# A wider product for the high softmax weights of a block's first query tile, with its low part added by VectorE

## The chip, the cores and the metric

The kernel runs on one core of a Trainium2 chip. The metric is the device time of one execution in microseconds (us); three executions of the kernel before took 2311.84, 2314.03 and 2314.23 us, so its median is 2314.03 us. A further execution was recorded by the profiler, and all durations below are from it: 2309.51 us, of which 2307.7 us lie between the first and the last instruction (the span).

## The reference: what must be computed

One decoder layer with the normalisation behind each part: self-attention, cross-attention, and a feed-forward part. The cross-attention is nearly all of the work, and the change lies in it:

```python
qh = _split_heads(jnp.einsum('bnq,qi->bni', x, Wq))        # 8 heads of 128, 16*112 = 1792 queries
kh = _split_heads(jnp.einsum('bmc,ci->bmi', context, Wk))  # 16*375 = 6000 keys
vh = _split_heads(jnp.einsum('bmc,ci->bmi', context, Wv))
sim = jnp.einsum('hid,hjd->hij', qh, kh) * SCALE
mean = jnp.mean(sim, axis=-1, keepdims=True)
sim = (sim - mean) * ATTN_MATRIX_SCALE + mean
attn = jax.nn.softmax(sim, axis=-1)
out = jnp.einsum('hij,hjd->hid', attn, vh)
```

The heads are split so that all batches of a head stand in one sequence: every one of a head's 1792 queries attends to all 6000 keys.

## The kernel before, in words

**Precision.** Values in float32 are written as a sum of two halves in float16, a high one and a low one. A product of two such values is three products on TensorE: high by high, high by low, low by high, all summed in PSUM. So the scores take `k_hi` by `q_hi`, `k_hi` by `q_lo` and `k_lo` by `q_hi` (line 416), and the output takes the softmax weights' high half `e_hi` by V's high half, `e_hi` by V's low half, and `e_lo` by V's high half (lines 440, 442 and 444).

**Tiling.** A head's queries are cut into 7 blocks of 256 (8 heads, so 56 blocks), a block into 2 query tiles of 128 (`t` is 0 and 1). The 6000 keys are 47 tiles of 128 (the last one of 112), taken in 12 groups `s` of four (three in the last). One group of one block is a step `f`: there are 672.

**One key tile of V** is a row of `VW` = 257 columns for each key: 128 of the high half, one column of ones (these 129 are `OW`), and 128 of the low half. The column of ones makes the sum of the weights come out as column 128 of the output. The output of a block stands in one PSUM bank, 4 or 5 by turns: two areas of 129 columns. For each key tile and each query tile TensorE loads `e_hi` and streams V's 129 high columns, loads `e_hi` again and streams V's 128 low columns into the first 128 columns of the same area, loads `e_lo` and streams the 129 high columns: 3 weight loads and 3 products, 386 columns.

**The pipeline of a step.** In step (n, s) TensorE first makes the scores of the step that lies 17 ahead (12 products of 256 columns, into one of two pairs of banks), then, in some steps, a side task (part of K, V or Q of the next head or block, lines 549, 559 and 566; at s = 8 the transposes and the spreading of the row maxima, lines 643 and 652), and then the attention products of its own step. ScalarE copies the scores into a ring in SBUF (line 839), later takes their exponential (line 854), and for even steps writes `e_hi` as well (line 846). VectorE folds the scores into a running maximum (line 1074, from PSUM) and subtracts the row maxima in the ring, 4 steps ahead (line 1095). GpSimd writes `e_hi` for odd steps (line 1596) and `e_lo` for all (line 1602; near the end VectorE takes the odd ones). Scores of a step wait until the running maximum has read the pair of banks two steps before; attention products wait for `e_lo`. The order on each engine is written out by hand in the program; nothing is scheduled by costs.

**The end of a block.** In step s = 1 of the next block VectorE inverts the two sums (`invert_sums`, line 1102), ScalarE copies the two tiles out of PSUM and scales them with the inverse into `o_buf` (`store_output`, line 878), and SyncE stores `o_buf` (`store`, line 1654). The semaphore of ScalarE's copies, `s_oev`, is what waits for a free bank or buffer go by: TensorE at the start of a block (line 754) and in the last part (line 697), VectorE's next `invert_sums`, and the store.

Of the kernel before, what the change touches and what calls it, by code (L numbers as in the profile page):

```python
# [7 lines left out]
ALU = mybir.AluOpType  # L8
ACT = mybir.ActivationFunctionType
# [10 lines left out]
NH, DH = 8, 128  # L20
# [16 lines left out]
VW = 2 * DH + 1  # L37
OW = DH + 1

SIM_SCALE = 1.5 * DH ** -0.5  # L40
# [28 lines left out]
def build(nc, xT, x, WA, Wo, ctxT, Wq, Wk, Wv, Wout, bout, W1T, b1, W2T, b2, o_dram, out):  # L69


    with ExitStack() as top:
# [158 lines left out]
        def batch_tokens(b, n=T):  # L231
# [26 lines left out]

        (s_qk, s_kept, s_max, s_sub, s_hi, s_exp, s_cast, s_lo, s_av, s_fold2, s_fold, s_bc, s_den, s_oev, s_od,
         s_init) = [  # L260
            sem("b_" + n) for n in ("qk", "kept", "max", "sub", "hi", "exp", "cast", "lo", "av", "fold2", "fold",
                                    "bc", "den", "oev", "od", "init")]

# [135 lines left out]
        with nc.Block() as block:  # L399

            @block.tensor
            def _(pe):
# [17 lines left out]
                def attend(f, more, more_sides):  # L420
# [12 lines left out]
                    for i in range(tiles_of(s)):  # L433
                        tile = s * GT + i
                        last_tile = tile == NKT - 1
                        keys = slice(0, LAST_KEYS if last_tile else P)
                        for t in range(QT):
                            cols = slice(i * QB + t * P, i * QB + (t + 1) * P)
                            out_t = psum[:, 4 + n % 2, t * OW:(t + 1) * OW]
                            pe.matmul(out_t, lhsT=e_hi_f[keys, cols], rhs=v_f[keys, i, 0:OW],  # L440
                                      start=(s == 0 and i == 0 and t == 0), stop=False)
                            pe.matmul(out_t[:, 0:DH], lhsT=e_hi_f[keys, cols], rhs=v_f[keys, i, OW:VW],  # L442
                                      start=False, stop=False)
                            mm = pe.matmul(out_t, lhsT=e_lo_f[keys, cols], rhs=v_f[keys, i, 0:OW],  # L444
                                           start=False, stop=last_tile and t == QT - 1)
# [245 lines left out]
                def n_transposes(p):  # L691
                    pe.wait_ge(t_n, 2 * p + 2)
                    if p:
                        pe.wait_ge(t_yl, p)
                    else:

                        pe.wait_ge(s_oev, NBLK * QT)
                    for r in range(2):
# [38 lines left out]
                def step(n, s, past=0):  # L737
# [13 lines left out]
                    if n >= 0:  # L751
                        if s == 0 and n >= 2:

                            pe.wait_ge(s_oev, n_at * QT - QT)
                        attend(n * NGRP + s, past * NQB * NGRP, past * HEAD_SIDES)
# [74 lines left out]
            def _(a):  # L830
# [42 lines left out]
                def store_output(n):  # L873
# [3 lines left out]
                    for t in range(QT):  # L877
                        a.activation(o_buf[:, t, :], psum[:, 4 + n % 2, t * OW:t * OW + DH], ACT.Copy,
                                     scale=o_den[:, t:t + 1]).then_inc(s_oev, 1)
# [180 lines left out]
            def _(v):  # L1060
# [37 lines left out]
                def invert_sums(n):  # L1098
                    v.wait_ge(s_av, n * NGRP + NGRP)
                    if n > 0:  # L1100
                        v.wait_ge(s_oev, n * QT)
                    v.reciprocal(o_den[:, :], psum[:, 4 + n % 2, 0:QT * OW].rearrange(
                        "p (t w) -> p t w", t=QT)[:, :, DH]).then_inc(s_den, 1)

# [289 lines left out]
                for f, n, s in steps():  # L1394
# [14 lines left out]
                    if task is not None:  # L1409
                        if task[0] != "t":  # L1410
                            halves += 1
                            low_half(n, s, halves)
                        number += 1
                    if s == MAX_S and n + 1 < NBLK:
                        fold_max(n + 1)
# [10 lines left out]
                invert_sums(NBLK - 1)  # L1426
                first_residual(1)
                second_statistics(0)
                o_low(5)
# [186 lines left out]
            def _(sp):  # L1616
# [35 lines left out]
                def store(h, qb):  # L1652
                    sp.wait_ge(s_oev, (h * NQB + qb + 1) * QT)
                    sp.dma_start(o_part[qb * QB:(qb + 1) * QB, h * DH:(h + 1) * DH].rearrange(
# [88 lines left out]
```

## Time and profile before

| | value |
|---|---|
| median of three executions | 2314.03 us (2311.84 to 2314.23) |
| profiled execution, its own time | 2309.51 us |
| its span | 2307.7 us |
| TensorE busy / weight loads busy | 98% / 88% |
| VectorE, ScalarE, GpSimd busy | 87%, 81%, 82% |
| granted TensorE clock | 1.000 over the whole span (2.4 GHz) |
| DMA | mean 22 GB/s |

A busy share is an average over the whole span, and matmuls overlap each other: a product of 128 columns is shown with 0.22 us although the next one starts 0.06 us behind it. What a product costs in a stream is the distance from its start to the next one's start. In the rows, PE is TensorE's products, PEld its weight loads, DVE VectorE, ACT ScalarE, POOL GpSimd.

### The profile page before, as it was taken

The numbers are of one execution on the slowest core, as the hardware profiler recorded it, in microseconds if no ns is written. First come the engines' busy times: TensorE is split into PE (matmuls) and PEld (weight loads), VectorE is DVE, ScalarE is ACT, GpSimd is POOL, SyncE is SP. The second block draws the span as 40 slices with busy tenths as digits, with TensorE's granted clock in tenths as the row PEclk, the third lists the DMA queues.
The fourth block names the chain that finished last, engine by engine and source line by source line (L and its number), as shares of the span: only waits on it lengthen the run. The fifth ranks groups of instructions, "written<-read, shape, count | busy, mean of one in ns | idle before, by whom it ended". The sixth has DMA issues, their size and how long they took to land.

```text
span 2307.7 us, 67182 instructions
## 1 busy us (share of the span) xinstructions
PE 2256.0 (98%) x28710; PEld 2022.1 (88%) x28710; DVE 2006.9 (87%) x2185; ACT 1867.3 (81%) x2224; POOL 1899.0 (82%) x1153
## 2 busy tenths in 40 slices
PE   7998999999999999999999999999999999999998
PEld 4568998899989998999889998999889998999886
DVE  8978888888889888888888888888898888888876
ACT  4457888888888888888878888888888888888855
POOL 8765888888878888888878897888878888899953
PEclk9999999999999999999999999999999999999999
DMA  6410000000000000000000000000000000010220
GB/s 201 157 51 2 7 4 13 7 4 6 11 6 5 6 13 4 6 4 7 13 4 7 4 13 4 6 7 4 13 4 6 7 4 6 4 47 6 94 76 33
DMA packets 34858, 50.79 MB, mean 22 GB/s; under 512 B 2304, under 2 KB 27392, under 8 KB 34560
## 3 DMA queue, kind: packets, MB, share of 16 engines
q1 hardware_dynamic: 34560, 46.46, 6.5%
q8 instruction: 230, 3.77, 0.7%
q14 instruction: 68, 0.56, 0.1%
HBM read 30.99 MB, written 15.47 MB: 20 GB/s over the span
## 4 chain that ended last, share of the span: by engine, by line
PE 71%; POOL 14%; DVE 7%; issue 4%; ACT 4%; POOLq 0%; ACTq 0%; DVEq 0%
PE psum L416 27%; POOL e_lo L1602 11%; PE psum L442 9%; PE psum L440 9%; PE psum L444 9%; PE psum L559 4%; PE psum L549 4%; POOL e_hi L1596 3%; DVE run_max L1074 3%; ACT ring L839 2%; PE psum L685 2%; PE psum L732 1%; PE psum L566 1%; PE psum L521 1%; PE psum L712 1%
## 5 line engine op out<-in xcount | busy, mean ns | idle before, releaser
L1602 POOL TENSOR_TENSOR e_lo<-ring,e_hi 128x1024 f16<-128x1024 f32 (+1 forms) x665 | 1388.8, 2103 | 196.8 <-ACT ring L854 168.4
L1074 DVE TENSOR_TENSOR run_max<-psum,run_max 128x1024 f16<-128x1024 f32 (+1 forms) x616 | 737.9, 1198 | 201.5 <-ACT ring L839 200.5
L839 ACT ACTIVATE ring<-psum 128x1024 f32<-128x1024 f32 (+1 forms) x672 | 673.7, 1003 | 181.5 <-PE psum L416 121.4
L1095 DVE SCALAR_TENSOR_TENSOR ring<-ring,psum 128x1024 f32<-128x1024 f32 (+1 forms) x672 | 792.5, 1186 | 0.7 <-PE psum L652 0.7
L416 PE MATMUL psum<-qx_hi,k_hi 128*128 128x256 f16 x2632 | 717.5, 273 | 14.9 <-DVE qx_lo L1062 5.9
L440 PE MATMUL psum<-v_main,e_hi 128*128 128x129 f16 x4032 | 717.7, 219 | 1.1 <-POOL e_lo L1602 1.1
L442 PE MATMUL psum<-v_main,e_hi 128*128 128x128 f16 x4032 | 718.3, 221 | 0.0
L416 PE MATMUL psum<-qx_hi,k_lo 128*128 128x256 f16 x2632 | 717.3, 273 | 0.0
L416 PE MATMUL psum<-qx_lo,k_hi 128*128 128x256 f16 x2632 | 717.2, 273 | 0.0
L444 PE MATMUL psum<-v_main,e_lo 128*128 128x129 f16 x4032 | 716.2, 218 | 0.0
L854 ACT ACTIVATE ring<-ring 128x1024 f32<-128x1024 f32 (+1 forms) x672 | 695.9, 1036 | 1.3 <-DVE ring L1095 0.7
L1596 POOL CAST e_hi<-ring 128x1024 f16<-128x1024 f32 x336 | 340.6, 1014 | 117.5 <-ACT ring L854 114.0
L846 ACT ACTIVATE e_hi<-ring 128x1024 f16<-128x1024 f32 x336 | 353.9, 1053 | 97.8 <-DVE ring L1095 96.9
L444 PEld LDWEIGHTS psum<-v_main,e_lo 128*128 128x128 f16 x4032 | 398.1, 99 | 0.0
L442 PEld LDWEIGHTS psum<-v_main,e_hi 128*128 128x128 f16 x4032 | 391.0, 97 | 7.1
L440 PEld LDWEIGHTS psum<-v_main,e_hi 128*128 128x128 f16 x4032 | 387.9, 96 | 8.5 <-issue 1.0
L416 PEld LDWEIGHTS psum<-qx_hi,k_hi 128*128 128x128 f16 x2632 | 257.1, 98 | 47.1 <-DVE run_max L1074 10.8
L416 PEld LDWEIGHTS psum<-qx_hi,k_lo 128*128 128x128 f16 x2632 | 257.4, 98 | 30.1
L416 PEld LDWEIGHTS psum<-qx_lo,k_hi 128*128 128x128 f16 x2632 | 257.4, 98 | 27.0
L440 PE MATMUL psum<-v_tail,e_hi 128*128 128x129 f16 (+1 forms) x1232 | 219.9, 219 | 0.4 <-POOL e_lo L1602 0.3
L442 PE MATMUL psum<-v_tail,e_hi 128*128 128x128 f16 (+1 forms) x1232 | 220.2, 221 | 0.0
L444 PE MATMUL psum<-v_tail,e_lo 128*128 128x129 f16 (+1 forms) x1232 | 219.5, 218 | 0.0
(198 smaller groups left out, 2760.8 us busy)
## 6 DMA issues: line engine op xcount, KB each, us to landing
o_scratch<-o_buf SPq DMA_DIRECT2D x56, 128.0 KB, 1.9
raw<-o_scratch SPq DMA_DIRECT2D x14, 512.0 KB, 3.7
stage<-in_ctxT SPq DMA_DIRECT2D x6, 500.0 KB, 3.9
stage<-in_ctxT SPq DMA_DIRECT2D x12, 250.0 KB, 4.8
w_scratch<-wall SPq DMA_DIRECT2D x1, 2304.0 KB, 9.7
wall<-w_scratch SPq DMA_DIRECT2D x6, 384.0 KB, 3.5
x<-in_xT SPq DMA_DIRECT2D x4, 448.0 KB, 6.1
res<-in_x SPq DMA_DIRECT2D x1, 1792.0 KB, 15.1
```

Source lines behind the costliest of these rows:

```text
L416: mm = pe.matmul(psum[:, 2 * (f % 2) + i // 2, (i % 2) * QB:(i % 2 + 1) * QB], lhsT=k[:, keys], rhs=q[:, qpar, :], start=(n == 0), stop=(n ...
L440: pe.matmul(out_t, lhsT=e_hi_f[keys, cols], rhs=v_f[keys, i, 0:OW], start=(s == 0 and i == 0 and t == 0), stop=False)
L442: pe.matmul(out_t[:, 0:DH], lhsT=e_hi_f[keys, cols], rhs=v_f[keys, i, OW:VW], start=False, stop=False)
L444: mm = pe.matmul(out_t, lhsT=e_lo_f[keys, cols], rhs=v_f[keys, i, 0:OW], start=False, stop=last_tile and t == QT - 1)
L549: mm = pe.matmul(psum[:, bank, 0:n], lhsT=w, rhs=y[:, c * KC:c * KC + n], start=(x == 0), stop=(x == 4))
L839: a.activation(ring[:, f % SLOTS, 0:n], pair(f)[:, 0:n], ACT.Copy).then_inc(s_kept, 1)
L846: a.activation(e_hi[f % NEH][:, 0:n], ring[:, f % SLOTS, 0:n], ACT.Exp, scale=SIM_SCALE).then_inc(s_hi, 1)
L854: a.activation(slot, slot, ACT.Exp, scale=SIM_SCALE).then_inc(s_exp, 1)
L1074: ins = v.tensor_tensor(run_max[:, 0:n], pair(f)[:, 0:n], run_max[:, 0:n], ALU.max)
L1095: v.scalar_tensor_tensor(slot, slot, LIFT, psum[:, 6, 0:QB].unsqueeze(1).broadcast_to([P, t, QB]), ALU.add, ALU.subtract).then_inc(s_sub, 1)
L1596: g.tensor_copy(e_hi[f % NEH][:, 0:n], slot).then_inc(s_cast, 1)
L1602: g.tensor_tensor(e_lo[f % NEL][:, 0:n], slot, e_hi[f % NEH][:, 0:n], ALU.subtract).then_inc(s_lo, 1)
```

## The change

For the first query tile of a block (`t` = 0) the first two products become one: `e_hi` is loaded once and V's whole row of 257 columns is streamed. The low part (128 columns) then no longer falls on top of the high part but stands in columns 129 to 256 of the bank; the second query tile's area moves from column 129 to column 258. Its three products stay as they are. Since the low part is now apart, it must be scaled and added: `add_low` does this on VectorE, behind ScalarE's copy of the high part, into `o_buf`. It is placed in step s = 2, behind that step's other work; for the last block it stands behind `first_residual(1)`. Its semaphore `s_olo` takes the place of `s_oev` in all four waits named above.

```diff
+O_AT = (0, VW + 1)
...
-                            out_t = psum[:, 4 + n % 2, t * OW:(t + 1) * OW]
-                            pe.matmul(out_t, lhsT=e_hi_f[keys, cols], rhs=v_f[keys, i, 0:OW],
-                                      start=(s == 0 and i == 0 and t == 0), stop=False)
-                            pe.matmul(out_t[:, 0:DH], lhsT=e_hi_f[keys, cols], rhs=v_f[keys, i, OW:VW],
-                                      start=False, stop=False)
+                            out_t = psum[:, 4 + n % 2, O_AT[t]:O_AT[t] + OW]
+                            if t == 0:
+                                pe.matmul(psum[:, 4 + n % 2, 0:VW], lhsT=e_hi_f[keys, cols], rhs=v_f[keys, i, :],
+                                          start=(s == 0 and i == 0), stop=False)
+                            else:
+                                pe.matmul(out_t, lhsT=e_hi_f[keys, cols], rhs=v_f[keys, i, 0:OW],
+                                          start=False, stop=False)
+                                pe.matmul(out_t[:, 0:DH], lhsT=e_hi_f[keys, cols], rhs=v_f[keys, i, OW:VW],
+                                          start=False, stop=False)
...
-                        pe.wait_ge(s_oev, NBLK * QT)
+                        pe.wait_ge(s_olo, NBLK)
...
-                            pe.wait_ge(s_oev, n_at * QT - QT)
+                            pe.wait_ge(s_olo, n_at - 1)
...
-                        a.activation(o_buf[:, t, :], psum[:, 4 + n % 2, t * OW:t * OW + DH], ACT.Copy,
+                        a.activation(o_buf[:, t, :], psum[:, 4 + n % 2, O_AT[t]:O_AT[t] + DH], ACT.Copy,
...
-                        v.wait_ge(s_oev, n * QT)
-                    v.reciprocal(o_den[:, :], psum[:, 4 + n % 2, 0:QT * OW].rearrange(
-                        "p (t w) -> p t w", t=QT)[:, :, DH]).then_inc(s_den, 1)
+                        v.wait_ge(s_olo, n)
+                    v.reciprocal(o_den[:, :], psum[:, 4 + n % 2, DH:O_AT[1] + OW:O_AT[1]]).then_inc(s_den, 1)
+
+                def add_low(n):
+
+                    v.wait_ge(s_oev, n * QT + QT)
+                    v.scalar_tensor_tensor(o_buf[:, 0, :], psum[:, 4 + n % 2, OW:VW], o_den[:, 0:1], o_buf[:, 0, :],
+                                           ALU.mult, ALU.add).then_inc(s_olo, 1)
...
+                    if s == 2 and n > 0:
+                        add_low(n - 1)
...
                 first_residual(1)
+                add_low(NBLK - 1)
...
-                    sp.wait_ge(s_oev, (h * NQB + qb + 1) * QT)
+                    sp.wait_ge(s_olo, h * NQB + qb + 1)
```

On TensorE, the products of the first two key tiles of a step (here the first of the program) stood so before; each row names the moving tile, the weights and the size:

```order
L440 MATMUL psum<-v_main_106,e_hi_112 128x129
L442 MATMUL psum<-v_main_106,e_hi_112 128x128
L444 MATMUL psum<-v_main_106,e_lo_116 128x129
L440 MATMUL psum<-v_main_106,e_hi_112 128x129
L442 MATMUL psum<-v_main_106,e_hi_112 128x128
L444 MATMUL psum<-v_main_106,e_lo_116 128x129
```

and stand so now:

```order
L445 MATMUL psum<-v_main_106,e_hi_112 128x257
L452 MATMUL psum<-v_main_106,e_lo_116 128x129
L448 MATMUL psum<-v_main_106,e_hi_112 128x129
L450 MATMUL psum<-v_main_106,e_hi_112 128x128
L452 MATMUL psum<-v_main_106,e_lo_116 128x129
```

Six products and six loads of a key tile have become five and five; the columns are the same, 772.

On VectorE, from the inverse in step s = 1 to the work of step s = 3, in a block that makes part of the next head's V, the order was:

```order
L1102 RECIPROCAL o_den<-psum 128x2 [waits b_oev,b_av]
L1095 SCALAR_TENSOR_TENSOR ring<-ring,psum 128x1024 [waits b_bc]
L1074 TENSOR_TENSOR run_max<-psum,run_max 128x1024 [waits b_max,b_kept]
L1095 SCALAR_TENSOR_TENSOR ring<-ring,psum 128x1024 [waits b_bc]
L1074 TENSOR_TENSOR run_max<-psum,run_max 128x1024 [waits b_max,b_kept]
L1062 SCALAR_TENSOR_TENSOR v_main_107<-psum,v_main_107 128x4x128 [waits b_half]
L1095 SCALAR_TENSOR_TENSOR ring<-ring,psum 128x1024 [waits b_bc]
L1074 TENSOR_TENSOR run_max<-psum,run_max 128x1024 [waits b_max,b_kept]
```

and is now:

```order
L1110 RECIPROCAL o_den<-psum 128x2 [waits b_olo,b_av]
L1103 SCALAR_TENSOR_TENSOR ring<-ring,psum 128x1024 [waits b_bc]
L1082 TENSOR_TENSOR run_max<-psum,run_max 128x1024 [waits b_max,b_kept]
L1103 SCALAR_TENSOR_TENSOR ring<-ring,psum 128x1024 [waits b_bc]
L1082 TENSOR_TENSOR run_max<-psum,run_max 128x1024 [waits b_max,b_kept]
L1070 SCALAR_TENSOR_TENSOR v_main_107<-psum,v_main_107 128x4x128 [waits b_half]
L1115 SCALAR_TENSOR_TENSOR o_buf<-psum,o_den,o_buf 128x128 [waits b_oev]
L1103 SCALAR_TENSOR_TENSOR ring<-ring,psum 128x1024 [waits b_bc]
L1082 TENSOR_TENSOR run_max<-psum,run_max 128x1024 [waits b_max,b_kept]
```

One instruction is new, the sum into `o_buf`; it stands ahead of step s = 3's subtraction and running maximum, and nothing else has changed its place.

## Rows read from the trace of the kernel before

**Rows 1.** The page: engines, the chain's shares, weight loads of the attention products.

```profile
PE 2256.0 (98%) x28710; PEld 2022.1 (88%) x28710; DVE 2006.9 (87%) x2185; ACT 1867.3 (81%) x2224; POOL 1899.0 (82%) x1153
...
PE 71%; POOL 14%; DVE 7%; issue 4%; ACT 4%; POOLq 0%; ACTq 0%; DVEq 0%
...
L444 PEld LDWEIGHTS psum<-v_main,e_lo 128*128 128x128 f16 x4032 | 398.1, 99 | 0.0
L442 PEld LDWEIGHTS psum<-v_main,e_hi 128*128 128x128 f16 x4032 | 391.0, 97 | 7.1
L440 PEld LDWEIGHTS psum<-v_main,e_hi 128*128 128x128 f16 x4032 | 387.9, 96 | 8.5 <-issue 1.0
```

**Rows 2.** Windows of one block each: length, busy us of each engine, clock.

```profile
1001.60:1037.30 35.70, 35.70 (x495) 34.03 (x493) 31.38 (x33) 30.82 (x37) 30.88 (x19) 1.00 0.02 6
2057.70:2091.30 33.60, 33.00 (x438) 30.81 (x436) 29.75 (x31) 29.06 (x34) 31.08 (x19) 1.00 0.22 76
```

**Rows 3.** Waits of TensorE's products from 237 to 2158 us: total, times, longest.

```profile
PE psum L416 <- DVE qx_lo L1062: 5.9, 14, 0.5
PE psum L416 <- issue: 2.8, 1, 2.8
PE psum L549 <- DVE k_lo L1062: 2.3, 7, 0.4
PE psum L416 <- DVE run_max L1074: 1.4, 4, 0.8
PE psum L652 <- DVE row_max L1087: 0.9, 3, 0.3
```

**Rows 4.** The same from 2158 to 2214 us, the last two blocks.

```profile
PE psum L643 <- DVE fold L1082: 1.9, 1, 1.9
PE psum L440 <- POOL e_lo L1602: 1.4, 3, 0.9
```

**Rows 5.** TensorE's order in time: start us, shown duration us, instruction.

```profile
1003.93 0.28 PE L559 MATMUL psum<-wall,ctx_hi 128*128 128x128 f16 x2
...
1005.04 0.22 PE L440 MATMUL psum<-v_main,e_hi 128*128 128x129 f16 x1
1005.10 0.22 PE L442 MATMUL psum<-v_main,e_hi 128*128 128x128 f16 x1
1005.16 0.22 PE L444 MATMUL psum<-v_main,e_lo 128*128 128x129 f16 x1
...
1006.42 0.27 PE L416 MATMUL psum<-qx_hi,k_hi 128*128 128x256 f16 x1
...
1007.73 0.22 PE L440 MATMUL psum<-v_main,e_hi 128*128 128x129 f16 x1
```

**Rows 6.** VectorE's order in time in steps s = 1 to 3 of a block.

```profile
1001.57 0.16 DVE L1102 RECIPROCAL o_den<-psum 128x2 f32<-128x2 f32 x1
...
1006.96 0.68 DVE L1062 SCALAR_TENSOR_TENSOR v_main<-psum,v_main 128x512 f16<-128x512 f32 x1
1007.55 1.21 DVE L1095 SCALAR_TENSOR_TENSOR ring<-ring,psum 128x1024 f32<-128x1024 f32 x1
1009.11 1.22 DVE L1074 TENSOR_TENSOR run_max<-psum,run_max 128x1024 f16<-128x1024 f32 x1 [0.34 <-ACT ring L839]
```

**Rows 7.** ScalarE's order in time, the copies out of PSUM and the next.

```profile
1004.03 0.62 ACT L878 ACTIVATE o_buf<-psum,o_den 128x128 f32<-128x128 f32 x2
```

**Rows 8.** VectorE's groups by form: count, busy us, mean ns, idle before.

```profile
L1062 DVE SCALAR_TENSOR_TENSOR v_main<-psum,v_main 128x512 f16<-128x512 f32 x72 | 48.9, 680 | 0.3 <-ACT v_main L871 0.3
L1062 DVE SCALAR_TENSOR_TENSOR qx_lo<-psum,qx_hi 128x256 f16<-128x256 f32 x56 | 23.1, 412 | 0.3 <-ACT qx_hi L931 0.3
L1102 DVE RECIPROCAL o_den<-psum 128x2 f32<-128x2 f32 x56 | 8.9, 158 | 0.0
```

**Rows 9.** VectorE and ScalarE in time behind the last block.

```profile
2213.51 0.15 DVE L1102 RECIPROCAL o_den<-psum 128x2 f32<-128x2 f32 x1
2213.70 0.62 ACT L878 ACTIVATE o_buf<-psum,o_den 128x128 f32<-128x128 f32 x2 [2.75 <-DVE o_den L1102]
...
2214.77 0.75 DVE L1308 BATCH_NORM_STATS2 bn<-res 128x6 f32<-128x256 f32 x2
2215.56 0.38 DVE L1313 BATCH_NORM_AGGREGATE mean<-bn 128x2 f32<-128x6 f32 x4
```

**Rows 10.** Waits from 2213 us on, for the products of line 700.

```profile
PEld psum L700 <- DVE norm L1327: 0.2, 1, 0.2
```

More of the change, by code:

```diff
@@ L253, in build @@
         s_lo_odd = sem("b_lo_odd")
-        (s_qk, s_kept, s_max, s_sub, s_hi, s_exp, s_cast, s_lo, s_av, s_fold2, s_fold, s_bc, s_den, s_oev, s_od,
+        (s_qk, s_kept, s_max, s_sub, s_hi, s_exp, s_cast, s_lo, s_av, s_fold2, s_fold, s_bc, s_den, s_oev, s_olo, s_od,
          s_init) = [
             sem("b_" + n) for n in ("qk", "kept", "max", "sub", "hi", "exp", "cast", "lo", "av", "fold2", "fold",
-                                    "bc", "den", "oev", "od", "init")]
+                                    "bc", "den", "oev", "olo", "od", "init")]
         s_side, s_half, s_free = sem("b_side"), sem("b_half"), sem("b_free")
```

## The prediction, before the changed kernel was run

> **What bounds the kernel now.** I read four views. First the page's busy shares and the chain: TensorE is busy 98% of the span, the others 81 to 87%, and 71% of the chain that ended last is TensorE, with 14% GpSimd [rows 1]. A share is an average, so next the windows of single blocks: in a common block TensorE is busy for all of its 35.7 us, VectorE for 31.4, ScalarE for 30.8, GpSimd for 30.9; in a late block without side tasks TensorE has 33.0 of 33.6 us, GpSimd, the next one, 31.1 [rows 2]. Third the waits: in the 1921 us from the first block's inverse to the last but one block (53 of the 56 blocks), TensorE's products wait 13.3 us in all, in 29 places, of which 2.8 us is one single gap in which no engine is waited for (issue) [rows 3]. So a stretch of TensorE time that goes away in this part goes away from the kernel, as long as no other engine needs 35 us for a block. Last the order in time, to see what a product costs in a stream, which its shown duration does not tell.
>
> **The saving on TensorE.** Distances between starts [rows 5]: the 12 score products of 256 columns from 1006.42 to 1007.73 us take 1.31 us, 109.2 ns each. 256 columns at 2.4 GHz (the granted clock is 1.00 [rows 2]) are 106.7 ns, so each product has about 2.5 ns over its columns. The 20 side products of 128 columns from 1003.93 to 1005.04 us take 1.11 us, 55.5 ns each: 53.3 and about 2.3. Weights are loaded for every one of these, and a load is shown with 96 to 99 ns [rows 1], longer than the 55.5 ns from product to product: it lies beside the products. The 24 attention products from 1005.04 to 1006.42 us take 1.38 us, 57.5 ns each, 172.5 for the three of one query tile and one key tile. Three plain ones of 129, 128 and 129 columns would be 56.0, 55.5 and 56.0, 167.5: one of the three costs about 5 ns more than its columns and its fixed part.
>
> After the change the three are two: 257 columns are 107.1 + 2.5 = 109.6 ns, and 129 columns 56.0, together 165.6 if the 5 ns go too, 170.6 if they stay. So the saving lies between 1.9 and 6.9 ns a key tile. Which one? The rows with two decimals do not show behind which product the 5 ns lie. But `e_lo`'s load is the longest of the three, 99 ns against 97 and 96 [rows 1], and it must be hidden under line 442's product of 128 columns, the shortest; under a product of 256 columns nothing of a load of that kind is seen (109.2 is columns and fixed part). The new order puts `e_lo`'s load under 257 columns. I take 6.5 ns, near the upper end: the rounding of the starts leaves about 1 ns open. There are 47 key tiles and 56 blocks, 2632 pairs: 2632 x 6.5 = 17.1 us. By the ends it is 5.0 and 18.2 us.
>
> A rule speaks against this. The Trainium skill, TensorE: Matmul & The Clock Gate, section "Wait — 56ns, not 53.3ns?", says that a warm product costs its columns at 2.4 GHz and a fixed part of about 2.5 ns, whatever its width. By that alone the change takes out one fixed part, 2632 x 2.5 = 6.6 us, and no more. The trace agrees for 256 and for 128 columns, and disagrees for the attention products by the 5 ns above. The same page, section "Back-to-back issue gap", gives about 81 ns for a product of 128 columns in a stream of loads and products, and 131 ns for 512. On a line between these a product of 257 columns would be 98 ns, and 162 ns would become 98: 168 us saved. The rows show 55.5 and 57.5 ns where it has 81, so I give this nearly nothing.
>
> **The added sum on VectorE.** 56 instructions with 128 columns, one input in PSUM, one in SBUF, output in SBUF. The trace has no such size; the same kind takes 680 ns with 512 columns and 412 with 256 [rows 8], so on the line through both 278 ns with 128. The inverse of two columns takes 158 ns [rows 8], a floor; 412 is the ceiling. An instruction's place in VectorE's queue is some 0.09 us less than its shown duration (line 1062 from 1006.96, the next from 1007.55, 0.59 for 0.68 [rows 6]): I take 0.19 us, 10.6 us in all, between 0.07 and 0.33 each. It stands where line 1095 starts at 1007.55 us. Queued behind it are the subtraction of s = 3 and the running maximum of s = 3, and in front of the latter VectorE idles 0.34 us for ScalarE's copy of the scores, which depends on TensorE alone [rows 6]. So 0.19 us, and 0.33 too, end in that gap: cost nothing. Only the subtraction comes 0.19 us later; its exponential belongs to a step four ahead.
>
> Its wait for ScalarE's two copies: they start at 1004.03 us and take 0.62 us [rows 7]; VectorE reaches the sum at about 1007.55, 2.9 us later. No wait. The ends that now go by the sum: TensorE at the start of the block after (ten steps later), the next inverse (11 steps), SyncE's store (3 us later, with a whole block until ScalarE writes `o_buf` again). Nothing.
>
> Behind the last block the sum stands behind `first_residual(1)`. ScalarE's copies end at 2214.32 us, the statistics before it only at 2215.52 [rows 9]: no wait, 0.19 us in front of a chain on which TensorE already waits 0.2 us once [rows 10]. I count +0.2 us. The store and the loads of tiles 10 to 13 queued behind it on SyncE start 1.3 us later; these tiles are transposed far behind the first ones, and TensorE has other products until then.
>
> **What is late next.** In the 28 places of rows 3 where TensorE waits for VectorE, the release comes from an earlier step of TensorE's own by way of ScalarE and VectorE, whose times stay. TensorE is 4 x 6.5 = 26 ns a step earlier there and waits that much longer: 28 x 0.026 = 0.7 us given back. In the last two blocks TensorE waits 1.9 us for the fold and 1.4 us in three places for `e_lo` [rows 4]; there GpSimd sets the pace for part of the way, so I count the gain of these two blocks (2 x 47 x 6.5 ns = 0.6 us) as lost.
>
> **Sum.** 17.1 - 0.7 - 0.6 - 0.2 = 15.6 us, 2309.5 - 15.6 = 2293.9 us for an execution like the profiled one. The median of the runs lies 4.5 us above it (2314.0), so the prediction is 2314.0 - 15.6 = 2298.4 us, 0.7% faster. Its own range is a saving from 12 to 19 us, 2295 to 2302.
>
> **Rivals.** About 0.2%, 4.6 us, is what a measurement of this kernel can tell from no change.
>
> 1. *The 5 ns stay.* If they belong to the stream of V's low half or to the accumulation, and not to `e_lo`'s load, the saving is the fixed part of one product, 2632 x 2.4 = 6.3 us, less 0.5: 2308.2 us. For it speaks that the rows do not show where the 5 ns lie, and the page's rule; against it that the load behind is the longest one.
>
> 2. *Another engine takes over the pace.* GpSimd needs 31.1 us of a late block's 33.6, and 14% of the chain is its [rows 1, 2]. If in truth its pace or the chain score, copy, maximum, score sets the block, the freed time is idle on TensorE and the time stays at 2314.0 us. Against it: a common block has not one wait of TensorE, and the waits of rows 3 are only in 28 places.
>
> 3. *Slower: the sum holds VectorE up.* Place: s = 2 of every block. If the sum takes (or waits) longer than the gap of 0.34 us, the running maximum comes late, then TensorE's scores. It decides from about 0.64 us on (the gap and the 0.30 us that a block gains). With 0.8 us for it, 55 x (0.8 - 0.34) = 25 us against 17: 2322 us. Against it: 412 ns is the ceiling from the same kind with twice the columns, and the copies are done 2.9 us before.
>
> 4. *More than forecast*, about 25 us: if weight loads held up the attention products in another way than I see, as by the page's 81 ns, the halved loads of `e_hi` would give more. 2289 us.
>
> **How the numbers follow.** Forecast 66%, rival 1 15%, rival 2 9%, rival 3 5%, rival 4 5%. The range goes from 2294 to 2310: it holds the forecast's own range with a margin for the upper bound of 18.2, and rival 1. It leaves out rivals 2, 3 and 4 and a few per cent of the others, some 20%. Faster by over 0.2%: the forecast, rival 4 and most of rival 1, 84%. Within 0.2%: rival 2 and the rest of rival 1, 11%. Slower: 5%.
>
> **What would show it.** In the profile after: the distance from a 257-column product to the next of 109.6 ns, and with 129 columns 165.6 for both (170.6 by rival 1); the group of a step at 1.35 us where it was 1.38; a common block of 35.4 us where it was 35.7, still with TensorE busy for all of it; line 1115's sum at about 0.28 us, and a gap before the running maximum of s = 3 down from 0.34 to about 0.12; TensorE's waits in the middle blocks up by no more than 1 us. The prediction is wrong if a common block shows waits of TensorE for `e_lo` or the running maximum, or if the wide product takes more than 112 ns.

## The result, and the profile after

Nine executions of the changed kernel took 2306.85 us in the median (2305.36 to 2308.08), nine of the kernel before 2313.98 us (2309.28 to 2315.32). The ratio is 0.9972 with a 95% interval of 0.9964 to 0.998: faster by 0.3%, 7.1 us. The sign holds, and so does the stated range of 2294 to 2310 us, but only by the room that it leaves for rival 1: the forecast's own range of 12 to 19 us does not hold. The size is off, 7.1 us in place of 15.6.

The page of the changed kernel, the lines that answer to [rows 1]; "L445" is now the wide product, "L448", "L450" and "L452" are the second tile's high, its low, and `e_lo`'s products:

```profile
PE 2252.5 (98%) x26078; PEld 1980.7 (86%) x26078; DVE 2020.4 (88%) x2241; ACT 1865.1 (81%) x2224; POOL 1898.6 (82%) x1153
...
PE 71%; POOL 15%; DVE 6%; issue 4%; ACT 3%; POOLq 0%; DVEq 0%; ACTq 0%
...
L452 PEld LDWEIGHTS psum<-v_main,e_lo 128*128 128x128 f16 x4032 | 395.8, 98 | 7.1
```

2632 products and as many loads have gone (28710 to 26078), and VectorE has 56 instructions more. TensorE's order in time in one step, as in [rows 5]:

```profile
1005.63 0.27 PE L445 MATMUL psum<-v_main,e_hi 128*128 128x257 f16 x1
1005.74 0.22 PE L452 MATMUL psum<-v_main,e_lo 128*128 128x129 f16 x1
1005.80 0.22 PE L448 MATMUL psum<-v_main,e_hi 128*128 128x129 f16 x1
1005.86 0.22 PE L450 MATMUL psum<-v_main,e_hi 128*128 128x128 f16 x1
1005.92 0.22 PE L452 MATMUL psum<-v_main,e_lo 128*128 128x129 f16 x1
...
1006.99 0.27 PE L420 MATMUL psum<-qx_hi,k_hi 128*128 128x256 f16 x1
```

The 20 products take 1.36 us, from 1005.63 to 1006.99; the 24 of before took 1.38. Rows with two decimals don't part such products; the mean over all full steps does. For each run I took the distance from each product's start to the next one's, at its place in the step, over 612 full steps of a trace (the last product of a step is left out, since what follows it is other work):

```
mean ns to the next start, by place             e_hi.V               e_lo | e_hi.V        e_lo | a key tile, both query tiles
before          (129, 128, 129 | 129, 128, 129) 56.3 59.7            55.9 | 56.1 59.7     55.9 | 343.6
after           (257, 129 | 129, 128, 129)      109.6                56.8 | 57.1 60.1     55.9 | 339.5
```

The period of a block shows as the distance from one inverse of VectorE to the next. Before, in the middle and at the end:

```profile
1073.14 0.16 DVE L1102 RECIPROCAL o_den<-psum 128x2 f32<-128x2 f32 x1
1108.93 0.16 DVE L1102 RECIPROCAL o_den<-psum 128x2 f32<-128x2 f32 x1
1143.52 0.16 DVE L1102 RECIPROCAL o_den<-psum 128x2 f32<-128x2 f32 x1
...
2057.73 0.16 DVE L1102 RECIPROCAL o_den<-psum 128x2 f32<-128x2 f32 x1
2091.27 0.16 DVE L1102 RECIPROCAL o_den<-psum 128x2 f32<-128x2 f32 x1
```

and after:

```profile
1073.41 0.16 DVE L1110 RECIPROCAL o_den<-psum 128x2 f32<-128x2 f32 x1
1108.98 0.16 DVE L1110 RECIPROCAL o_den<-psum 128x2 f32<-128x2 f32 x1
1143.58 0.16 DVE L1110 RECIPROCAL o_den<-psum 128x2 f32<-128x2 f32 x1
...
2055.25 0.16 DVE L1110 RECIPROCAL o_den<-psum 128x2 f32<-128x2 f32 x1
2088.78 0.16 DVE L1110 RECIPROCAL o_den<-psum 128x2 f32<-128x2 f32 x1
```

A common block went from 35.79 to 35.57 us. The fourth block of a head did not move (34.59, now 34.60), nor did the late blocks without side tasks (33.54, now 33.53). That is the first finding: twelve of the 55 periods between inverses gave nothing (together 0.07 us), the seven fourth ones, the four of about 33.5 us and the one behind them.

The sum on VectorE, and what stands around it, as in [rows 6]:

```profile
1007.64 0.68 DVE L1070 SCALAR_TENSOR_TENSOR v_main<-psum,v_main 128x512 f16<-128x512 f32 x1
1008.24 0.34 DVE L1115 SCALAR_TENSOR_TENSOR o_buf<-psum,o_den,o_buf 128x128 f32<-128x128 f32 x1
1008.49 1.21 DVE L1103 SCALAR_TENSOR_TENSOR ring<-ring,psum 128x1024 f32<-128x1024 f32 x1
1009.79 1.23 DVE L1082 TENSOR_TENSOR run_max<-psum,run_max 128x1024 f16<-128x1024 f32 x1
```

It takes 0.34 us and its place 0.25; the gap of 0.34 us before the running maximum of s = 3 is down to 0.09 us (1008.49 + 1.21 to 1009.79).

The two profiled spans differ by only 2.6 us (2307.7 and 2305.1), because the stretch ahead of the first inverse took 237.2 us in the one and 241.5 in the other. The windows from 45 to 100 us, before and after, differ in the granted clock (the column behind GpSimd's):

```profile
45.00:100.00 55.00, 51.41 (x564) 26.61 (x561) 46.94 (x61) 20.09 (x24) 41.49 (x27) 1.00 0.61 196
```

```profile
45.00:100.00 55.00, 53.21 (x523) 26.70 (x524) 42.72 (x56) 19.02 (x23) 41.47 (x27) 0.88 0.61 196
```

A mean of 0.88 means part of this stretch at 1.2 GHz, here from 45.3 to 59.0 us. No kernel differs between 45 and 100 us, and the change alone does not bring it: in the eleven profiles below, the stretch ahead of the first inverse took 237.2 us once, for a variant of the changed kernel, and 240.6 to 242.4 us ten times, for variants of the kernel before too.

From the first inverse to the last, the kernel before takes 1976.36 us and the changed one 1969.37: 6.99 us less, close to the difference of the medians. In this part, too, the clock is not the same. Between the 28th and the 29th block TensorE stands idle for 2.8 us in the kernel before and for 2.5 in the changed one, and only in the changed one it then runs at 1.2 GHz, from 1219.5 to 1222.9 us. A window just behind the gap, before and after:

```profile
1219.80:1223.10 3.30, 3.30 (x43) 3.10 (x43) 0.82 (x1) 1.88 (x3) 1.01 (x1) 1.00 0.02 5
```

```profile
1219.60:1222.90 3.30, 3.30 (x22) 2.59 (x20) 0.26 (x1) 1.31 (x2) 0.99 (x1) 0.50 0.02 5
```

In the same 3.3 us 43 products start in the one and 22 in the other. What this costs is worked out in the section on why the prediction went as it did; without it the two traces would be 8.3 us apart (7.0 and 1.3). The part behind the last inverse is 94.2 us in both.

### The profile page after: what moved, and what is told of

It reads as the page before. It is cut to its first block, busy times and chain, and to the rows that moved or that the text cites. A ratio compares the mean times of both kernels' runs of the same rounds, so it can differ in the third digit from the quotient of the medians.

```text
span 2305.1 us, 61948 instructions
## 1 busy us (share of the span) xinstructions
PE 2252.5 (98%) x26078; PEld 1980.7 (86%) x26078; DVE 2020.4 (88%) x2241; ACT 1865.1 (81%) x2224; POOL 1898.6 (82%) x1153
## 4 chain that ended last, share of the span: by engine, by line
PE 71%; POOL 15%; DVE 6%; issue 4%; ACT 3%; POOLq 0%; DVEq 0%; ACTq 0%
PE psum L420 26%; POOL e_lo L1618 12%; PE psum L452 9%; PE psum L445 9%; PE psum L450 5%; PE psum L448 5%; PE psum L567 4%; PE psum L557 4%; POOL e_hi L1612 3%; DVE run_max L1082 3%; ACT ring L847 2%; PE psum L693 2%; PE psum L740 1%; PE psum L529 1%; PE psum L574 1%
## 5 line engine op out<-in xcount | busy, mean ns | idle before, releaser
L452 PE MATMUL psum<-v_main,e_lo 128*128 128x129 f16 x4032 | 711.4, 220 | 0.0
L445 PE MATMUL psum<-v_main,e_hi 128*128 128x257 f16 x2016 | 550.4, 273 | 1.3 <-POOL e_lo L1618 1.3
L450 PE MATMUL psum<-v_main,e_hi 128*128 128x128 f16 x2016 | 446.9, 222 | 0.0
L448 PE MATMUL psum<-v_main,e_hi 128*128 128x129 f16 x2016 | 445.7, 221 | 0.0
L452 PEld LDWEIGHTS psum<-v_main,e_lo 128*128 128x128 f16 x4032 | 395.8, 98 | 7.1
L448 PEld LDWEIGHTS psum<-v_main,e_hi 128*128 128x128 f16 x2016 | 197.5, 98 | 25.3
L452 PE MATMUL psum<-v_tail,e_lo 128*128 128x129 f16 (+1 forms) x1232 | 217.9, 219 | 0.0
L445 PEld LDWEIGHTS psum<-v_main,e_hi 128*128 128x128 f16 x2016 | 194.2, 96 | 8.7 <-issue 1.0
L450 PEld LDWEIGHTS psum<-v_main,e_hi 128*128 128x128 f16 x2016 | 197.7, 98 | 0.0
```

The lines of the kernel that those rows point to most:

```text
L445: pe.matmul(psum[:, 4 + n % 2, 0:VW], lhsT=e_hi_f[keys, cols], rhs=v_f[keys, i, :], start=(s == 0 and i == 0), stop=False)
```

## The experiments

**1. Does VectorE's sum cost anything?** The changed kernel without it:

```diff
-                    if s == 2 and n > 0:
-                        add_low(n - 1)
...
-                add_low(NBLK - 1)
```

(the waits on `s_olo`, left out here, go by `s_oev` again).

> The changed kernel without VectorE's sum (the low part of the first query tile is left out of the output); the four waits go by ScalarE's copies again. My theory: the sum costs nothing, since VectorE idles 0.34 us behind it in a common block: common blocks 35.57 us as in the changed kernel, late blocks 33.5, time as the changed kernel's, 7 us under the kernel before. Rival: the sum holds up the chain of scores: common blocks down to 35.4 us and late ones to 33.3, some 8 to 10 us more saved, 15 to 17 in all, which was the forecast.

Measured: 2306.92 us, ratio 0.9971 (0.9959 to 0.9982); common blocks 35.57, late ones 33.55, 1969.49 us from the first inverse to the last. All of it as with the sum, so the sum costs nothing in any block, as forecast.

**2. Who paces the blocks that did not move?** First TensorE was relieved by 2.8 us a block:

```diff
-                                pe.matmul(out_t[:, 0:DH], lhsT=e_hi_f[keys, cols], rhs=v_f[keys, i, OW:VW],
-                                          start=False, stop=False)
```

> The changed kernel without the low product of the second query tile (V's low half left out there): 47 products of 60 ns less in a block, 2.8 us of TensorE's time. My theory: the late blocks without side tasks are paced by GpSimd (its e_lo frees the ring slots that ScalarE's copies of scores wait for), not by TensorE, and stay at 33.5 us; common blocks fall only to that floor, from 35.57 to 33.5. Rival (TensorE sets the pace everywhere, with a few fixed waits): late blocks 33.5 - 2.8 = 30.7 us, common ones 32.8.

Measured: 2257.47 us in one execution. The inverses of this run, in the middle and at the end:

```profile
1050.77 0.16 DVE L1108 RECIPROCAL o_den<-psum 128x2 f32<-128x2 f32 x1
1085.73 0.16 DVE L1108 RECIPROCAL o_den<-psum 128x2 f32<-128x2 f32 x1
1120.31 0.17 DVE L1108 RECIPROCAL o_den<-psum 128x2 f32<-128x2 f32 x1
...
2040.85 0.16 DVE L1108 RECIPROCAL o_den<-psum 128x2 f32<-128x2 f32 x1
2074.37 0.16 DVE L1108 RECIPROCAL o_den<-psum 128x2 f32<-128x2 f32 x1
```

The late block stays at 33.52 us and the fourth one at 34.58: TensorE doesn't pace them. The common block fell to 34.96 and not to 33.5, as I had expected; so there another engine takes over only 0.6 us below where it now stands. The waits in two common blocks of this run (1015.8 to 1085.7 us) name GpSimd:

```profile
ACT ring L845 <- POOL e_lo L1616: 5.4, 8, 0.9
POOL e_lo L1616 <- ACT ring L860: 3.9, 2, 1.9
```

The first block gave nothing either: its inverse comes at 237.20 us here and at 237.15 in the kernel before, both at a clock of 1.00. Then GpSimd was burdened (the new semaphore is left out):

```diff
+                    if f % NGRP == 4:
+                        g.tensor_tensor(e_lo[f % NEL][:, 0:QB], slot[:, 0:QB], e_hi[f % NEH][:, 0:QB],
+                                        ALU.subtract).then_inc(s_again, 1)
+                        g.wait_ge(s_again, f // NGRP + 1)
```

> The changed kernel, in which GpSimd makes a quarter of one e_lo of every block twice, some 0.6 us more of its time in a block. My theory (in the late blocks, and in the fourth block of each head, GpSimd paces the others by the ring slots it frees): these 11 blocks grow from 33.53 and 34.60 by about 0.6 us, to 34.1 and up to 35.2; common blocks stay at 35.57, since TensorE paces them. Rival (TensorE and fixed waits pace all blocks): no block changes.

```profile
1076.56 0.16 DVE L1110 RECIPROCAL o_den<-psum 128x2 f32<-128x2 f32 x1
1112.13 0.16 DVE L1110 RECIPROCAL o_den<-psum 128x2 f32<-128x2 f32 x1
1147.42 0.16 DVE L1110 RECIPROCAL o_den<-psum 128x2 f32<-128x2 f32 x1
...
2061.68 0.16 DVE L1110 RECIPROCAL o_den<-psum 128x2 f32<-128x2 f32 x1
2095.88 0.16 DVE L1110 RECIPROCAL o_den<-psum 128x2 f32<-128x2 f32 x1
```

Measured: 2316.02 us in one execution; the second subtraction is shown with 0.67 us. The common block is 35.57 us as without the burden; the fourth one grew by 0.69 to 35.29, the late one by 0.67 to 34.20. So a block in which no attention product waits for GpSimd's `e_lo` is nevertheless paced by GpSimd. The waits of the changed kernel in two late blocks (2059.9 to 2122 us) show how it gets there:

```profile
ACT ring L847 <- POOL e_lo L1618: 5.5, 8, 0.9
POOL e_lo L1618 <- ACT ring L862: 3.9, 2, 1.9
ACT e_hi L854 <- DVE ring L1103: 3.4, 2, 1.7
PEld psum L420 <- DVE run_max L1082: 1.6, 4, 0.4
PEld psum L660 <- DVE row_max L1095: 1.0, 2, 0.5
PE psum L420 <- DVE run_max L1082: 0.9, 4, 0.2
PE psum L660 <- DVE row_max L1095: 0.7, 2, 0.3
```

ScalarE's copy of scores waits for a slot of the ring, which is free when GpSimd has made the `e_lo` of 16 steps before; the running maximum waits for the copy, TensorE's scores for the running maximum. At the start of a block GpSimd waits 1.9 us for exponentials, which need the row maxima. So the late period is GpSimd's 31.1 us of work [rows 2] and its waits. That the links on ScalarE and VectorE count as well is read from these waits; no run changed them. Of the waits on TensorE only small last links (0.9 and 0.7 us in two blocks) are seen.

**3. Where do the 5 ns of the attention products lie?** In the table above they stand behind the second product, V's low half on its own: 59.7 ns for 128 columns. The prediction gave them to `e_lo`'s load behind it. Two tests on the kernel before. First the order of the first two products was turned (except at a block's first key tile):

```diff
-                            pe.matmul(out_t, lhsT=e_hi_f[keys, cols], rhs=v_f[keys, i, 0:OW],
-                                      start=(s == 0 and i == 0 and t == 0), stop=False)
-                            pe.matmul(out_t[:, 0:DH], lhsT=e_hi_f[keys, cols], rhs=v_f[keys, i, OW:VW],
-                                      start=False, stop=False)
+                            first = s == 0 and i == 0
+                            for low in ((False, True) if first else (True, False)):
+                                pe.matmul(out_t[:, 0:DH] if low else out_t, lhsT=e_hi_f[keys, cols],
+                                          rhs=v_f[keys, i, OW:VW] if low else v_f[keys, i, 0:OW],
+                                          start=(first and t == 0 and not low), stop=False)
```

> The kernel before, with the first two products of each key and query tile in the other order (V's low half, then its high half and the ones), except for a block's first key tile. In the kernel before the distances are 56 ns behind the first product, 60 behind the second (V's low half), 56 behind the third. Theory A (the 4 to 5 ns belong to the load of e_lo, which must be hidden under the product just before it): 55.5 behind the low product, 60 behind the high one, 56 behind e_lo's, and blocks of 35.78 us as before. Theory B (they belong to the stream of V's low half wherever it stands): 60 behind the first product now, 56 behind the second; blocks of 35.78 us too.

Then the third product took `e_hi`'s weights again:

```diff
-                            mm = pe.matmul(out_t, lhsT=e_lo_f[keys, cols], rhs=v_f[keys, i, 0:OW],
+                            mm = pe.matmul(out_t, lhsT=e_hi_f[keys, cols], rhs=v_f[keys, i, 0:OW],
```

> The kernel before, whose third product takes e_hi's weights again in place of e_lo's (the low halves of the weights are left out of the output; they are still made and waited for). Theory A1 (e_lo's own place in SBUF makes its load longer): 55.5 ns behind the second product and common blocks 94 x 4.5 ns = 0.4 us shorter, 35.4. Theory A2 or B (the place in the order or the stream makes it, whatever the weights are): 60 ns and 35.78 us as before.

```
mean ns to the next start            first tile            second tile         a key tile
turned: low, high, e_lo              56.9  56.5  56.9      59.9  56.2  56.0    342.4
e_hi thrice: high, low, high         56.3  59.7  55.9      56.1  59.7  55.9    343.6
```

`e_hi` thrice changes nothing (2314.23 us): the weights' own place doesn't matter. Turned (2313.07 us), `e_lo`'s load lies under the high product and that takes 56.2 to 56.5 ns: it is not `e_lo`'s load. The low product keeps its 59.9 ns in the second tile; in the first it has 56.9 (by key tile of a step 56.8, 55.7, 59.2 and 55.8), so it isn't simply the low half's stream wherever it stands either. Both theories that I gave fall in part. The places where it is slow have in common that the product just before streams the high half of the same row of V; the first tile here is the only place where that is not so, and its third key tile is slow all the same, as is not every place of the first kind (experiment 4). No run tests this.

**4. V's rows start at odd multiples of 2 bytes.** A row of 257 columns of 2 bytes puts every second row, and the low half of every other one, beside a multiple of 4 bytes. In the kernel before the row was made 258 wide, with two columns of ones (products of 130, 128, 130); the buffers that lie behind V's in SBUF move by 64 to 160 bytes with it:

```diff
-VW = 2 * DH + 1
-OW = DH + 1
+VW = 2 * DH + 2
+OW = DH + 2
...
```

> The kernel before with V's row 258 wide: two columns of ones behind the high half, so the products are 130, 128 and 130 columns wide, all even, and every row of V starts at a multiple of 4 bytes. Plain costs (columns at 2.4 GHz and 2.5 ns) would be 4 x 56.7 + 2 x 55.8 = 338.4 ns for a key tile of both query tiles; the kernel before takes 343.6 against a plain 336.6. Theory O (odd widths or odd addresses cost the 7 ns): 338.4 ns, common blocks 47 x 5.2 ns = 0.24 us shorter, 35.54. Rival (a load that changes the weights, or the product of 128 columns itself, costs it): about 345 ns and blocks of 35.85 us.

And with the same row, but only 129 columns of it streamed:

```diff
-                            out_t = psum[:, 4 + n % 2, t * OW:(t + 1) * OW]
+                            out_t = psum[:, 4 + n % 2, t * OW:(t + 1) * OW - 1]
...
-rhs=v_f[keys, i, 0:OW]
+rhs=v_f[keys, i, 0:DH + 1]
```

> As the run with even products, V's row 258 wide, but one column of ones is streamed: products of 129, 128 and 129 columns with all starts at multiples of 4 bytes. If it is the odd width that costs: 343 to 344 ns for a key tile as in the kernel before, blocks of 35.78 us. If it is the odd start of V's rows or of the low half: the plain 336.6 ns, blocks of 35.45 us.

```
mean ns to the next start            first tile            second tile         a key tile   common block
258 wide row, 130, 128, 130          56.2  58.6  56.1      56.1  58.6  55.9    341.6        35.67 us
258 wide row, 129, 128, 129          56.1  58.6  56.0      56.1  58.6  55.8    341.1        35.67 us
```

2312.06 and 2310.24 us in one execution each. Neither figure that I gave came (336.6 or 343 to 344 ns for the second run). One column less in four of the products takes off only 0.5 ns; the new row takes off 2.5 ns a key tile, a third of the 7.0 ns over the plain cost of 336.6. I put it down to the start of V's rows; that the moved buffers have no part in it is not shown. The rest stays with the low product: in the wide row it takes 59.3 to 60.1 ns at the first three key tiles of a step and 55.5 to 55.9 at the fourth. In the row of 257 the fourth is slow too, 58.1 and 58.5.

**5. Both tiles wide.** A bank's row has 512 columns in the kernel's `psum` tensor and two wide products need 514, so the second tile's took 255, and its low part, which then lies apart, is left out of the output (the products that these replace are left out here):

```diff
-O_AT = (0, VW + 1)
+O_AT = (0, VW)
...
+                            wide = VW if t == 0 else VW - 2
+                            pe.matmul(psum[:, 4 + n % 2, O_AT[t]:O_AT[t] + wide], lhsT=e_hi_f[keys, cols],
+                                      rhs=v_f[keys, i, 0:wide], start=(s == 0 and i == 0 and t == 0), stop=False)
```

> The changed kernel, whose second query tile has a wide product too, of 255 columns (the last two columns of V's low half are left out for it, since a bank holds 512 columns and 514 would be needed; the low part of that tile lands apart and is not added, so it is left out of the output). Four products a key tile, 257, 129, 255 and 129 columns, none of 128. In the changed kernel the second tile's three take 173.1 ns where they took 171.7 before. If what lengthens them is the short low product (60.1 ns), this gives 109.6 + 56.8 + 108.8 + 56.8 = 332 ns for a key tile against 339.5, 0.35 us a common block: 35.2. If every product behind a wide one costs 1 to 2 ns more, 335 ns and 35.35. The 11 blocks paced by GpSimd stay at 34.60 and 33.53.

Measured: 2295.08 us; 110.0 and 56.5 ns, 109.6 and 58.4, together 334.5 a key tile; common blocks 35.30, the fourth 34.60, late ones 33.53. The second tile's wide product and `e_lo`'s take 168.0 ns in place of 173.1, of which 0.8 ns is the two columns left out. So a product of its own for the low half costs 4 to 5.5 ns more than its share of a wide one, in either tile, and something of 1 to 2 ns behind wide products remains (58.4 for `e_lo` in the second tile). Of my two figures the second was right.

**6. A version that beats both kernels.** The changed kernel with the row 258 wide, all outputs complete:

```diff
-VW = 2 * DH + 1
-OW = DH + 1
+VW = 2 * DH + 2
+OW = DH + 2
...
-O_AT = (0, VW + 1)
+O_AT = (0, VW)
...
```

> The changed kernel with V's row 258 wide: products of 258, 130, 130, 128 and 130 columns. Plain costs are 110.0 + 3 x 56.7 + 55.8 = 335.9 ns for a key tile; the changed kernel takes 339.5 against a plain 334.2. Theory O (odd widths or addresses cost 5.3 ns): 335.9 ns, common blocks 47 x 3.6 = 0.17 us shorter, 35.40, with some 43 such blocks 7 us less than the changed kernel, 14 us less than the kernel before (0.994). Rival: 341 ns and no gain on the changed kernel.

Measured: 2301.38 us in the median of five, ratio to the kernel before 0.9952 (0.9938 to 0.9966). A key tile takes 109.5 + 56.2 + 56.7 + 58.9 + 55.8 = 337.1 ns, the first tile's pair 165.6. It lies between my two figures (335.9 and 341 ns). Its inverses:

```profile
1071.14 0.16 DVE L1110 RECIPROCAL o_den<-psum 128x2 f32<-128x2 f32 x1
1106.62 0.16 DVE L1110 RECIPROCAL o_den<-psum 128x2 f32<-128x2 f32 x1
1141.23 0.16 DVE L1110 RECIPROCAL o_den<-psum 128x2 f32<-128x2 f32 x1
```

35.48 for a common block, 34.61 still for the fourth. Against the changed kernel the medians differ by 5.0 to 5.5 us, but by the two traces the 41 periods that moved at all give only 3.4 of it; 2.0 lie around the gap ahead of the 29th block, where this profile has a clock of 1.00 and the changed kernel's has not. With the second tile's low product moved ahead of its high one:

```diff
+                                for low in ((False, True) if s == 0 and i == 0 else (True, False)):
+                                    pe.matmul(out_t[:, 0:DH] if low else out_t, lhsT=e_hi_f[keys, cols],
+                                              rhs=v_f[keys, i, OW:VW] if low else v_f[keys, i, 0:OW],
+                                              start=False, stop=False)
```

> The changed kernel with V's row 258 wide (337.1 ns a key tile, 2301.4 us), and the second query tile's low product ahead of its high one. In the kernel before, this order gave 342.4 ns in place of 343.6. If the 59 ns of the low product come from what its stream meets behind a high product, they go down to 56 to 57 ns here and a key tile to 334 to 336 ns, common blocks from 35.48 to 35.40, 2299 us. If they belong to the stream of the low half, or to the second place among three, 337 ns and 2301 us.

Measured: 2301.06 us (four executions), ratio 0.9947 (0.993 to 0.9964); 58.7 ns for the low product, now the first of three, 56.1 for the high one ahead of `e_lo`'s load, 337.1 in all. Here the extra follows the low stream and not the place in the order, and again not `e_lo`'s load. The second of my two figures came (337 ns and 2301 us).

**7. The changed kernel once more**, beside the two last ones.

> The changed kernel itself, beside the variants, for a second profile and a second comparison: 0.997 of the kernel before; common blocks 35.57 us, late ones 33.53. The stretch ahead of the first block's inverse took 237.2 us in the profile of before and 241.5 in the changed kernel's, with a lower granted clock from 45 to 100 us. If that comes from the change, it is 241.5 again; if it is chance, it can be either.

Measured: 2306.4 us (2302.43 to 2307.95, eight executions), ratio 0.997 (0.996 to 0.9981); 339.5 ns a key tile; blocks of 35.57, 34.60 and 33.55; 241.05 us ahead of the first inverse.

## Why the prediction was right in sign and wrong in size

The steps in its order.

*TensorE paces the kernel, so what goes there goes from the time.* Right for the common blocks and wrong for thirteen: the fourth block of each of the first seven heads, the four late ones whose period is 33.5 us, the one after (28.78 us, now 28.79), and the first block (experiment 2). I read the waits of TensorE, found 28 small ones, and took them as fixed delays that grow by 26 ns each. The 21 for Q and K did so, by some 0.03 us each. In a block whose pace another engine sets, though, TensorE's small waits take in everything that it gains. Rival 2 named the engine and the chain, but as all or nothing; in truth it held in 12 blocks of 56 (who paces the first one I did not look up). It could have been read in the trace of before, in the waits of ScalarE's copies for a slot of the ring: in a common block (1001.6 to 1037.3 us), a fourth one (1108.9 to 1143.5) and two late ones (2057 to 2124) they are

```profile
ACT ring L839 <- POOL e_lo L1602: 0.6, 1, 0.6
...
ACT ring L839 <- POOL e_lo L1602: 2.5, 4, 0.9
...
ACT ring L839 <- POOL e_lo L1602: 5.5, 8, 0.9
```

and experiment 2 shows that 2.8 us less for TensorE moves such blocks by nothing. Price: 13 x 47 x 4.1 ns = 2.5 us.

*A pair of products saves 6.5 ns.* This is the step that failed most. The wide product costs 109.6 ns, exactly as computed. But the first tile's pair takes 166.4, not 165.6, in place of 171.9, not 172.5 (that was the rounding of the starts): 5.5 ns. And the second tile's three, which the prediction took as untouched, rose from 171.7 to 173.1. Net 4.1 ns, 2632 x 4.1 = 10.8 us in place of 17.1. The 5 ns did go with the separate low product, so rival 1 was right that `e_lo`'s load is not the cause, wrong that the 5 ns stay, and near in its time (2308.2 us) by luck; but the reason I gave, `e_lo`'s load, was wrong: experiments 3 and 6 put that load under another product, which then takes 56 ns. What makes a low product of its own slow, and what lengthens the products behind a wide one by about 1 ns, stays open; the wider row of V takes 2.4 to 2.5 ns off a key tile in both kernels and so explains nothing of the difference between them.

*Given back: 0.7 us of waits, 0.6 us in the last two blocks.* The last but one block gave nothing, the last one 0.18 us. The waits of TensorE's products in the changed kernel from 241 to 2158 us are

```profile
PE psum L420 <- DVE qx_lo L1070: 6.4, 14, 0.6
PE psum L420 <- DVE run_max L1082: 4.7, 8, 2.5
PE psum L557 <- DVE k_lo L1070: 2.5, 7, 0.4
PE psum L660 <- DVE row_max L1095: 1.7, 7, 0.3
```

against [rows 3]. Those for Q and K grew by 0.5 and 0.2 us, as forecast. Those for the row maxima and, without the single long one, for the running maximum grew by 0.8 us each; they lie in the fourth and the late blocks and take in the gain of those blocks.

*A term that the prediction does not have: the clock.* The single gap of 2.8 us, once "issue", now ends on the running maximum with 2.5 us. It lies where TensorE's program comes to its second turn of the loop over pairs of heads. The two periods around it take 77.37 us where they took 76.35. Their extra over their like elsewhere (the 34th and 35th period) falls into two groups. In six profiles it is 4.1 to 4.6 us, and in exactly these the granted clock is 0.50 for a while behind the gap: the changed kernel twice, experiment 1, the burden of experiment 2, and two variants of the kernel before (turned, and 258 wide with products of 130). In the other seven, the kernel before among them (3.0 us), it is 1.0 to 3.0 us, and the clock behind the gap stays at 1.00. So what grew between the two traces is the clock's, 4.36 - 3.02 = 1.3 us. The gap is not longer where the clock falls: it is 2.3 to 2.8 us there, and 2.0 to 2.8 us where it stays, the 2.8 being the kernel before. The executions as a whole point the same way: their mean clock is 0.9967 over 17 executions of the changed kernel and 0.9978 over 30 of the kernel before, and among those with 0.997 the medians are 2306.1 (5) and 2314.6 us (9), 8.5 apart. Whether the change itself makes the lower clock likelier no run here separates.

*The sum on VectorE costs nothing.* Right, and experiment 1 shows it. Its duration was 341 ns, not 278, its place 0.25 us, not 0.19; the place lies inside the gap of 0.34.

*The new waits and the end cost nothing, +0.2 us behind the last block.* 94.21 us behind the last inverse in both: nothing.

Together: 10.8 - 2.5 - 1.3 = 7.0 us, the 6.99 of the traces. Of the 8.6 us that the forecast of 15.6 was too high, 6.3 are the saving of a pair and its neighbours, the largest part by far; the two terms given back were 1.3 us and should have been 2.5, and the clock had no term. Neither of the two signs that I gave for being wrong came. Of those for being right, the pair (166.4 ns for 165.6) and the step (1.36 us for 1.35) came near; the common block (35.57 us for 35.4) did not, nor did TensorE's waits, which rose by 2.0 us and not by at most 1.

The rule of the Trainium skill on the fixed part of a product (TensorE: Matmul & The Clock Gate, section "Wait — 56ns, not 53.3ns?") gave 6.6 us, close to the 7.1 measured, but by luck and not for its reason. The trace has 109.6 for 257 columns as by the rule, and 60 ns where the rule has 55.8; the saving is 4.1 ns a pair in place of 2.5, and then a third of it is lost elsewhere. The 81 ns that the Trainium skill gives for 128 columns in a stream (same page, section "Back-to-back issue gap") are seen in no run here.

## What to carry to other kernels

Before a saving on the busiest engine is multiplied by the number of stages, take the period of each stage and ask for each one who sets it: equal periods with small waits of the busiest engine mean that another one does, and there the gain is nothing and not the gain less a little. A chain back through a ring of buffers hardly shows in the waits of the engine at its end, but it does in those of the engine that fills the ring; a run that relieves the busiest engine, and one that burdens the suspect, settle it. When two profiles are compared stretch by stretch, the granted clock of each stretch belongs beside it: here it would have hidden 1.3 us of the gain. And in a dense stream of products the neighbours of a changed product must be counted too: here they took back a quarter of what the pair saved.

## What the runs showed of the hardware that was not expected

- Two products with the same weights, 129 and 128 columns, take 116.0 ns in the first tile where one of 257 takes 109.6: about 6.4 ns and not the fixed 2.3 of one product.
- With V's rows at multiples of 4 bytes a key tile takes 341.1 (129 wide) or 341.6 ns (130 wide) in place of 343.6, and in the changed kernel 337.1 in place of 339.5. A wider row with an unused or doubled column was thus faster here; buffers behind it moved too, which no run separates.
- The same 55 us of self-attention run at a granted clock of 1.00 in some executions and at 0.88 to 0.91 in others, 4 us of an execution.
- Behind a gap of 2.0 to 2.8 us of TensorE at the same place of the program, the clock fell to 1.2 GHz in six of 13 profiles. Between the traces of the kernel before and of the changed one this is worth 1.3 us, so even from the first inverse on two profiles are not compared without their clocks.
